# A Mamba-2 mixer that works on two sequences by turns: two transposes and one product change places

## The chip, the cores and the metric

One core of one Trainium2 chip runs the whole kernel. The time is the device time of one execution in microseconds (us), and lower is better. VectorE, ScalarE, GpSimd, TensorE and the DMA queues each run their own list of instructions in order and wait for one another by semaphores.

## The reference

The block has two layers on x of shape (2, 4096, 256). The change lies in the first, a Mamba-2 mixer with a gated linear unit and a layer norm behind it; the second sends each token to 4 of 16 experts.

```
h = layernorm(x) * (1 + ca) + sa
z, xBC, dt = split(h @ W_in)                 # 512, 768, 8 columns
xs, B, C = split(silu(causal_conv4(xBC)))    # 512, 128, 128
state = state * exp(dt*A) + dt * xs (x) B    # 8 heads of 64 x 128, a scan over 4096 tokens
y = state . C + D_skip * xs
y = rmsnorm(y * silu(z)) * rms_w @ W_out + h
a, gate = split(y @ glu_w + glu_b);  y = y + a * sigmoid(gate)
x = x + ga * layernorm(y)
h = layernorm(x) * (1 + cb) + sb             # then the router and the experts
```

The scan is done in chunks of 128 tokens: inside a chunk by a matrix of decays times C.B (tile `dec`), across chunks by the state.

## The kernel before

The kernel has three parts: a first pass over all tokens (layer norm, dt, the sums of the decays), the mixer, and the experts. The mixer takes 256 tokens (two chunks, c = 0 and 1) of one of the two sequences at a time. It is a chain of "halves", written out by hand in `halves`. In a half, up to four groups of tokens are at different stages: `first` (projection and convolution begin), `second` (the scan), `tail` (output projection, gated unit, second norm) and `routed` (third norm, router). From step 4 on every half also has `chosen` or `placed` (the top-4 choice, in the first half of a step, and the assignment of rows, in the second), and `copied` and `sent` (eight indirect stores of 128 rows each on GpSimd's queue, line 1546). Each engine has its own `half` that says in which order it does its share. There are 32 halves with an `add_h`; steps 4 to 15 are twelve of the `chosen` kind and twelve of the `placed` kind, steps 2 and 3 and the half ahead of them have no row stores.

What the steps of this study are, by line:

- VectorE: `add_h` (1308) adds h to the output projection and is the mark from which offsets are counted here. `new_state` (1291) adds a chunk's contribution to the state. `gated` (1313, 1317) makes y of the gated unit, tile `y1`. `norm2` (1323, 1328, 1331) takes mean and variance of the transposed y from PSUM and writes `rs`. `times_decay` (1270) multiplies `dec` by C.B from `bg`. `scale_from_state` (1277), `add_within` (1285), `apply2` (1338, 1345).
- TensorE: `x_by_token` (845) transposes the convolved x of a chunk; `turn_x2` (962) transposes the normalised x of the third norm; `logits` (970) is the router; `b_by_token` (854, 857); `transpose_y2` (951) transposes y of the gated unit; `turn_rows` (982) transposes rows for the stores; `from_state` (905), `state_add` (912), `within` (890, 894).
- ScalarE: `copy_b` (1095) copies C.B and the transposed B to `bg`; `modulate` (1157) follows `turn_x2`.
- GpSimd: `decay_state` (1511) multiplies the state by its decay and stands behind the last six of the eight indirect stores. `shift_x` (1527) stands ahead of them.

The waits that matter:

```
times_decay:       dec_done (chunk c), btok_done          # ScalarE's decays and copy_b
from_state(c=0):   st_done, btok_done
decay_state:       yst_ps                                 # from_state's product
new_state:         add_ps (state_add), sdec_done (decay_state)
transpose_y2:      y2_done (gated), tanh_done
norm2:             y2T_ps (transpose_y2)
turn_x2:           xn_done (normalize), yTl_done, tanh2_done
x_by_token(c):     xs_done, zs_done
```

Of the kernel before, what the change touches and what calls it, by code (L numbers as in the profile page):

```python
# [521 lines left out]
def mixer(nc, sem, prime, clear_semaphores, t, mod, gate_b_row, gate_ln, ident, minus_half, bank, run, h_dram, h2_dram, par_dram,  # L522
          cs_dram, x2_dram, xs_dram):
    with ExitStack() as ctx:
# [184 lines left out]
        def Q(b, n):  # L709
            return bank[4 * b + n]  # L710
# [37 lines left out]
        with nc.Block() as block:  # L748
# [63 lines left out]
            def _(pe):  # L812
# [28 lines left out]
                def x_by_token(b, i, c):  # L841
                    pe.wait_ge(xs_done[b], 3 * i + 2)
                    pe.wait_ge(zs_done[b], CH * i + c + 1)
                    for m in range(KI):
                        last = pe.transpose(Q(b, c)[:, m * P:(m + 1) * P], cv[b][:, m, c * P:(c + 1) * P],
                                            ident[:, :])
                    last.then_inc(xT_ps[b], 1)
# [13 lines left out]
                def exponents(b, i, c):  # L861
                    pe.wait_ge(ends_in[c][b], 32 * (i + 1))
                    if c == 0:
                        pe.wait_ge(xc_done[b], 3 * i + 3)
                        pe.wait_ge(tap0_done[b], 3 * i + 3)
                        pe.wait_ge(st_done[b], CH * i)
                        if above_zero(i - 2):
                            pe.wait_ge(rows_done[b], i - 2)
                        if b == 1 and above_zero(i - 1):
                            pe.wait_ge(pos_read, i - 1)  # L870
                    else:
                        pe.wait_ge(dec_done[b], CH * i + c)

                    for half_heads in range(2):
                        pe.matmul(Q(b, 2 + half_heads)[:, :].rearrange("p (h i) -> p h i", h=4), far[:, :],
                                  after[:, :].unsqueeze(1).to_broadcast([P, 4, P]), start=True, stop=False,
                                  skip_group_check=True)
                    for half_heads in range(2):
                        heads = slice(half_heads * 4, half_heads * 4 + 4)
                        last = pe.matmul(Q(b, 2 + half_heads)[:, :], ends_j[c][:, :],  # L880
                                         ends_i[c][:, heads, :].rearrange("p h i -> p (h i)"),
                                         start=False, stop=True, skip_group_check=True)
                    last.then_inc(dec_ps[b], 1)
# [24 lines left out]
                def state_add(b, i, c):  # L908
                    pe.wait_ge(xend_done[b], CH * i + c + 1)
                    pe.wait_ge(btok_done[b], i + 1)  # L910
                    pe.wait_ge(dec_done[b], CH * i + CH)
                    pe.matmul(Q(b, 3)[:, :], bg[b][:, 0, c, :], xend[b][:, c, :],
                              start=True, stop=True).then_inc(add_ps[b], 1)
# [32 lines left out]
                def transpose_y2(b, i):  # L946
                    pe.wait_ge(y2_done[b], i + 1)
                    pe.wait_ge(tanh_done[b], i + 1)
                    for c in range(CH):
                        for k in range(KD):  # L950
                            last = pe.transpose(Q(b, 1)[:, c * D + k * P:c * D + (k + 1) * P],
                                                y1[b][:, k, c * P:(c + 1) * P], ident[:, :])
                    last.then_inc(y2T_ps[b], 1)
# [48 lines left out]
                def half(first, second, tail, soon=None, routed=None, chosen=None, placed=None, copied=None, sent=None):  # L1002
                    if second:
                        project_z(*second, 1)
                    if tail:
                        project_out(*tail)
                    if second:
                        exponents(*second, 0)
                    if routed:
                        turn_x2(*routed)  # L1010
                    if second:
                        x_by_token(*second, 0)
                        x_by_token(*second, 1)
                    if tail:
                        state_add(*tail, 1)
                    if routed:
                        logits(*routed)
                    if tail:
                        glu(*tail)
                    if second:  # L1020
                        exponents(*second, 1)
                    if first:
                        project_xbc(*first, 0)
                    if second:
                        b_by_token(*second)
                    if tail:
                        transpose_y2(*tail)
                    if copied:
                        turn_rows(*copied)
                    if second:  # L1030
                        from_state(*second, 0)
                        state_add(*second, 0)
                        within(*second, 0)
                        from_state(*second, 1)
                        within(*second, 1)
                    if first:
                        project_xbc(*first, 1)
                        project_xbc(*first, 2)
                    if chosen:
                        positions(*chosen)  # L1040
                    if second:
                        transpose_y(*second, 0)
                    if first:
                        project_z(*first, 0)
                    if second:
                        transpose_y(*second, 1)

                halves(pe, half)


# [180 lines left out]
            def _(dve):  # L1231
# [79 lines left out]
                def gated(b, i):  # L1311
                    dve.wait_ge(tanh_done[b], i + 1)
                    dve.scalar_tensor_tensor(sg[b][:, :, :], sg[b][:, :, :], 1.0, half_a[b][:, :, :],
                                             ALU.add, ALU.mult).then_inc(ag_done[b], 1)
                    dve.wait_ge(ag_done[b], i + 1)
                    dve.wait_ge(y1l_done[b], i + 1)
                    dve.tensor_tensor(y1[b][:, :, :], y1[b][:, :, :], sg[b][:, :, :], ALU.add).then_inc(y2_done[b], 1)
# [117 lines left out]
                def half(first, second, tail, soon=None, routed=None, chosen=None, placed=None, copied=None, sent=None):  # L1435
                    if routed:
                        shift_of_norm3(*routed)
                    if tail:
                        add_h(*tail)
                    if second:  # L1440
                        conv(*second, 2)
                    if tail:
                        new_state(*tail, 1)
                    if second:
                        for c in range(CH):
                            times_dt(*second, c)
                            times_end(*second, c)
                    if chosen:
                        choose(*chosen)
                    if placed:  # L1450
                        assign(*placed)
                    if tail:
                        gated(*tail)
                    if tail:
                        norm2(*tail)
                    if second:
                        times_decay(*second, 0)
                        scale_from_state(*second, 0)
                        new_state(*second, 0)
                        times_decay(*second, 1)  # L1460
                        add_within(*second, 0)
                        scale_from_state(*second, 1)
                    if tail:
                        apply2(*tail)
                    if second:
                        mean_square(*second, 0)
                        add_within(*second, 1)
                    if first:
                        conv(*first, 0)
                    if second:  # L1470
                        mean_square(*second, 1)
                        split_yT(*second, 0)
                    if tail:
                        norm3_stats(*tail)
                    if second:
                        split_yT(*second, 1)
                    if tail:
                        norm3_aggr(*tail)
                    if first:
                        conv(*first, 1)  # L1480
                    if chosen:
                        read_positions(*chosen)

                halves(dve, half)


# [738 lines left out]
```

## Time and profile before

| | us |
|---|---|
| median of 3 runs | 1934.55 (1931.98 to 1934.59) |
| the profiled execution, its own time | 1935.59 |
| its span, first to last instruction | 1933.8 |
| TensorE busy in the span | 1616.6 (84%) |
| VectorE busy | 1336.5 (69%) |
| ScalarE busy | 1114.8 (58%) |
| GpSimd busy | 1000.9 (52%) |

The span is that of one profiled execution; the time of an execution is 1.8 us more than its span. Busy time counts an instruction from its start to its end, and neighbours on one engine overlap by up to some 0.1 us. The mixer's halves begin at about 200 us and the last `add_h` is at 1223.69.

### The profile page before, as it was taken

To read this page: it belongs to the slowest core of one execution; us is meant where nothing else is said; L and a number is where in the kernel's file an instruction comes from. 1 tells how busy PE (TensorE), PEld (TensorE's weight loads), DVE (VectorE), ACT (ScalarE), POOL (GpSimd) and SP (SyncE) were. 2 spreads that over 40 slices of the span, in tenths; PEclk is the share of its full clock that TensorE was granted. 3 is DMA by queue.
4 is the path that set the end of the run, shared out by engine and by line. 5 is a ranking of instruction groups with operands and counts; after the bars stand their busy time and mean duration, and the time that the engine had idled before them with its cause. 6 is when DMAs were issued, how large, how long until landed. Compare 5 with 4: busy or idle time off the path is not lost. (4 is left out here: it accounts for less than half of the span.)

```text
span 1933.8 us, 35775 instructions
## 1 busy us (share of the span) xinstructions
PE 1616.6 (84%) x10868; PEld 1388.4 (72%) x10868; DVE 1336.5 (69%) x3159; ACT 1114.8 (58%) x2270; POOL 1000.9 (52%) x954
## 2 busy tenths in 40 slices
PE   6753999999999999999999999501999999994777
PEld 6743777777777777777777777401999999993554
DVE  6642778888888888888888888414555555552777
ACT  2323575767676767676767676313777776772211
POOL 1201334556566565656565655654566666663432
PEclk8556999999999999999999999655999999997999
DMA  7412011112222121222222211237565665657995
GB/s 250 153 65 63 16 38 36 55 63 74 66 71 69 59 81 59 77 63 70 69 69 69 71 60 66 74 107 225 163 192 182 184 187 180 183 175 261 397 375 211
DMA packets 146311, 238.21 MB, mean 123 GB/s; under 512 B 25644, under 2 KB 92588, under 8 KB 145872
## 3 DMA queue, kind: packets, MB, share of 16 engines
q1 hardware_dynamic: 120016, 164.30, 26.7%
q0 software_dynamic: 26112, 71.62, 10.4%
q8 instruction: 97, 1.59, 0.4%
q14 instruction: 86, 0.70, 0.1%
HBM read 126.36 MB, written 109.48 MB: 122 GB/s over the span
## 5 line engine op out<-in xcount | busy, mean ns | idle before, releaser
L1930 POOL DMA_INDIRECT ys_dram<-byo,bids x272 | 260.8, 959 | 158.2 <-ACT byo L1863 115.3
L1244 DVE SCALAR_TENSOR_TENSOR cv<-xc,convw,cv 128x256 f32<-128x256 f32 x576 | 300.3, 588 | 35.1 <-ACT cv L1071 35.1
L1546 POOL DMA_INDIRECT xs_dram<-rows,dest x256 | 258.0, 1008 | 73.9 <-issue 70.7
L1896 DVE TENSOR_TENSOR bff<-bgs,bank 128x256 f32<-128x256 f32 x136 | 57.2, 421 | 166.4 <-ACT bgs L1847 164.6
L118 PE MATMUL bank<-wh,bhh 128*128 x544 | 157.4, 289 | 1.9 <-issue 1.2
L119 PE MATMUL bank<-wl,bhh 128*128 x544 | 154.8, 284 | 0.0
L120 PE MATMUL bank<-wh,bhl 128*128 x544 | 154.1, 283 | 0.0
L118 PE MATMUL bank<-hTh,win_hi 128*128 128x256 f32 x384 | 116.4, 303 | 36.3 <-POOL hTl L1504 32.9
L1110 ACT ACTIVATE xdt<-yy 128x512 f32<-128x512 f32 x64 | 40.2, 629 | 161.8 <-POOL yy L1517 161.8
L1517 POOL TENSOR_TENSOR yy<-yy,zs 128x512 f32<-128x512 f32 x64 | 87.8, 1371 | 72.4 <-DVE yy L1285 71.9
L1863 ACT ACTIVATE byo<-bank,bx 128x256 f32<-128x256 f32 x272 | 114.1, 471 | 17.1 <-PE bank L120 1.4
L894 PE MATMUL bank<-xdt,dec 128*128 128x64 f32 x1024 | 121.6, 272 | 1.7 <-DVE dec L1270 1.7
L894 PEld LDWEIGHTS bank<-xdt,dec 128*128 128x128 f32 x1024 | 119.5, 192 | 2.1 <-DVE dec L1270 2.1
L1773 PE MATMUL bank<-ident,bx 128*128 128x128 f32 x544 | 83.8, 277 | 36.0 <-DMA bx<-xs_dram 35.9
L1887 DVE TENSOR_TENSOR bhl<-bank,bhh 128x512 fp32r<-128x512 f32 x136 | 94.0, 691 | 26.0 <-ACT bhh L1840 12.1
L118 PEld LDWEIGHTS bank<-hTh,win_hi 128*128 128x128 f32 x384 | 74.1, 193 | 51.4 <-issue 44.7
L120 PE MATMUL bank<-hTh,win_lo 128*128 128x256 f32 x384 | 109.8, 286 | 0.0
L119 PE MATMUL bank<-hTl,win_hi 128*128 128x256 f32 x384 | 109.8, 286 | 0.0
L118 PEld LDWEIGHTS bank<-wh,bhh 128*128 128x128 f32 x544 | 103.3, 190 | 6.5 <-issue 6.1
L1071 ACT ACTIVATE cv<-bank,convb,convw 128x256 f32<-128x256 f32 x192 | 97.6, 562 | 11.4 <-PE bank L120 11.4
L1847 ACT ACTIVATE bgs<-bank 128x256 f32<-128x256 f32 x136 | 52.2, 383 | 89.5 <-PE bank L120 89.5
L119 PEld LDWEIGHTS bank<-wl,bhh 128*128 128x128 f32 x544 | 103.4, 190 | 0.0
(263 smaller groups left out, 5387.3 us busy)
## 6 DMA issues: line engine op xcount, KB each, us to landing
bx<-xs_dram SPq DMA_DIRECT2D x272, 129.0 KB
cy<-ys_dram SPq DMA_DIRECT2D x32, 1024.0 KB, 10.8
px<-in_x SPq DMA_DIRECT2D x16, 512.0 KB, 3.6
h_t<-phT SPq DMA_DIRECT2D x16, 512.0 KB, 4.1
hT<-h_t SPq DMA_DIRECT2D x32, 256.0 KB, 2.7
xr<-in_x SPq DMA_DIRECT2D x32, 256.0 KB, 2.7
x_dram<-xr SPq DMA_DIRECT2D x32, 256.0 KB, 2.0
h_dram<-h SPq DMA_DIRECT2D x32, 256.0 KB, 2.5
```

The source lines that it names most:

```text
L118: pe.matmul(out, a_hi, b_hi, start=start, stop=False, skip_group_check=True)
L119: pe.matmul(out, a_hi, b_lo, start=False, stop=False, skip_group_check=True)
L120: return pe.matmul(out, a_lo, b_hi, start=False, stop=stop, skip_group_check=True)
L894: last = pe.matmul(Q(b, c)[:, h * HD:(h + 1) * HD], dec[b][:, c, h, :], xdt[b][:, c, h * HD:(h + 1) * HD], start=False, stop=True, skip_gr ...
L1071: last = act.activation(cv[b][:, n, :], Q(b, pair)[:, m * GROUP:(m + 1) * GROUP], ACT.Identity, bias=convb[:, n:n + 1], scale=convw[:, n, ...
L1244: dve.scalar_tensor_tensor(cv[b][:, m, :], xc[b][:, m, tap:tap + GROUP], convw[:, m, tap:tap + 1], cv[b][:, m, :], ALU.mult, ALU.add).then ...
L1517: pool.tensor_tensor(y, y, zs[b][:, c, :], ALU.mult).then_inc(y4_done[b], 1)
L1546: pool.indirect_dma_start(out=xs_dram[:, :], out_offset=bass.IndirectOffsetOnAxis(ap=dest[p][:, CH * b + c, k:k + 1], axis=0), in_=rows[b] ...
L1773: last = pe.transpose(XT[u % 2][:, (k * 2 + n) * P:(k * 2 + n + 1) * P], x[u % XBUF][:, n, k * P:(k + 1) * P], ident[:, :])
L1863: last = act.activation(yo[u % YBUF][:, n, :], DN[u % 2][:, n * D:(n + 1) * D], ACT.Copy, scale=x[u % XBUF][:, n, D + 1:D + 2])
L1887: dve.tensor_tensor(hl[u % 2][:, :, :, :].rearrange("p k n t -> p (k n t)"), XT[u % 2][:, :], hh[u % 2][:, :, :, :].rearrange("p k n t -> ...
L1930: pool.indirect_dma_start(out=ys_dram[:, :], out_offset=bass.IndirectOffsetOnAxis(ap=ids[u % XBUF][:, n:n + 1], axis=0), in_=yo[u % YBUF][ ...
```

## The change

Three steps change places, in TensorE's and VectorE's order of work. No instruction, tile or wait is added or taken away.

- TensorE turns the normalised x (`turn_x2`) between the two `x_by_token` and no longer ahead of both.
- TensorE turns y (`transpose_y2`) behind `turn_rows`, the first `from_state` and the first `state_add`, and no longer ahead of the three.
- VectorE does the first `times_decay` ahead of `norm2` and no longer behind it.

```diff
--- before.py
+++ after.py
@@ -1006,10 +1006,11 @@
                         project_out(*tail)
                     if second:
                         exponents(*second, 0)
+                    if second:
+                        x_by_token(*second, 0)
                     if routed:
                         turn_x2(*routed)
                     if second:
-                        x_by_token(*second, 0)
                         x_by_token(*second, 1)
                     if tail:
                         state_add(*tail, 1)
@@ -1023,13 +1024,14 @@
                         project_xbc(*first, 0)
                     if second:
                         b_by_token(*second)
+                    if copied:
+                        turn_rows(*copied)
+                    if second:
+                        from_state(*second, 0)
+                        state_add(*second, 0)
                     if tail:
                         transpose_y2(*tail)
-                    if copied:
-                        turn_rows(*copied)
-                    if second:
-                        from_state(*second, 0)
-                        state_add(*second, 0)
+                    if second:
                         within(*second, 0)
                         from_state(*second, 1)
                         within(*second, 1)
@@ -1451,10 +1453,11 @@
                         assign(*placed)
                     if tail:
                         gated(*tail)
+                    if second:
+                        times_decay(*second, 0)
                     if tail:
                         norm2(*tail)
                     if second:
-                        times_decay(*second, 0)
                         scale_from_state(*second, 0)
                         new_state(*second, 0)
                         times_decay(*second, 1)
```

## Rows read from the trace of the kernel before

**Rows 1.** Busy time by stage, mixer: us, each engine's busy us (count), PEclk, DMA.
```profile
200.00:1224.00 1024.00, 952.69 (x6435) 790.31 (x6435) 866.32 (x2083) 708.74 (x1405) 581.23 (x554) 0.99 0.19 62
```

**Rows 2.** Timeline, VectorE, a chosen half: start, us, line, tiles, [idle before].
```profile
700.00 0.69 DVE L1308 TENSOR_TENSOR y<-bank,hT 128x512 f32<-128x512 f32 x1 [0.41 <-PE bank L120]
...
711.80 0.69 DVE L1317 TENSOR_TENSOR y<-y,sg 128x512 f32<-128x512 f32 x1
...
713.24 0.76 DVE L1323 BATCH_NORM_STATS2 st<-bank 128x6 f32<-128x256 f32 x2 [0.75 <-PE bank L951]
...
714.43 0.17 DVE L1331 TENSOR_SCALAR rs<-mv 128x2 f32<-128x2 f32 x1
...
714.51 1.22 DVE L1270 TENSOR_TENSOR dec<-dec,bg 128x1024 f32<-128x1024 f32 x1
...
715.65 0.68 DVE L1277 TENSOR_TENSOR yy<-bank,par 128x512 f32<-128x512 f32 x1
...
716.74 0.69 DVE L1291 TENSOR_TENSOR state<-state,bank 128x512 f32<-128x512 f32 x1 [0.41 <-POOL state L1511]
...
733.14 0.69 DVE L1308 TENSOR_TENSOR y<-bank,hT 128x512 f32<-128x512 f32 x1 [0.27 <-PE bank L120]
```

**Rows 3.** Timeline, GpSimd, the same half.
```profile
712.91 0.96 POOL L1546 DMA_INDIRECT xs_dram<-rows,dest  x1 [0.30 <-issue]
...
714.17 0.96 POOL L1546 DMA_INDIRECT xs_dram<-rows,dest  x1 [0.30 <-issue]
...
715.15 1.48 POOL L1511 TENSOR_TENSOR state<-state,par 128x512 f32<-128x512 f32 x1
```

**Rows 4.** Timeline, ScalarE and TensorE, the same half.
```profile
711.17 0.60 ACT L1095 ACTIVATE bg<-bank 128x512 f32<-128x512 f32 x1 [1.04 <-PE bank L857]
...
712.55 0.66 PE L951 MATMUL bank<-ident,y 128*128 128x128 f32 x4 [1.42 <-DVE y L1317]
```

**Rows 5.** Timeline, VectorE, the half behind it.
```profile
746.45 1.23 DVE L1270 TENSOR_TENSOR dec<-dec,bg 128x1024 f32<-128x1024 f32 x1
...
749.69 0.69 DVE L1291 TENSOR_TENSOR state<-state,bank 128x512 f32<-128x512 f32 x1 [1.42 <-POOL state L1511]
...
765.25 0.69 DVE L1308 TENSOR_TENSOR y<-bank,hT 128x512 f32<-128x512 f32 x1 [0.41 <-PE bank L120]
```

**Rows 6.** Timeline, GpSimd, the same half.
```profile
744.84 0.96 POOL L1546 DMA_INDIRECT xs_dram<-rows,dest  x1 [0.30 <-issue]
...
747.37 1.14 POOL L1546 DMA_INDIRECT xs_dram<-rows,dest  x1 [0.30 <-issue]
...
748.53 1.05 POOL L1511 TENSOR_TENSOR state<-state,par 128x512 f32<-128x512 f32 x1
```

**Rows 7.** Timeline, VectorE and TensorE, an early half without row stores.
```profile
277.31 0.69 DVE L1308 TENSOR_TENSOR y<-bank,hT 128x512 f32<-128x512 f32 x1 [0.41 <-PE bank L120]
...
289.23 1.10 PE L905 MATMUL bank<-state,cv 128*128 128x512 f32 x2 [0.34 <-ACT bg L1095]
...
291.02 1.05 PE L890 MATMUL bank<-skip_w,cv 128*128 128x128 f32 x8
...
292.42 0.69 DVE L1291 TENSOR_TENSOR state<-state,bank 128x512 f32<-128x512 f32 x1 [0.40 <-POOL state L1511]
...
308.28 0.69 DVE L1308 TENSOR_TENSOR y<-bank,hT 128x512 f32<-128x512 f32 x1 [0.41 <-PE bank L120]
```

**Rows 8.** Timeline, VectorE and GpSimd, four instructions where the two meet.
```profile
322.16 1.04 POOL L1511 TENSOR_TENSOR state<-state,par 128x512 f32<-128x512 f32 x1 [6.41 <-PE bank L905]
...
322.44 0.79 DVE L1331 TENSOR_SCALAR rs<-mv 128x2 f32<-128x2 f32 x1
...
648.23 2.63 DVE L1270 TENSOR_TENSOR dec<-dec,bg 128x1024 f32<-128x1024 f32 x1
...
709.49 0.41 DVE L1391 TENSOR_SCALAR mask<-mask 128x64 f32<-128x64 f32 x1
```

**Rows 9.** Timeline, TensorE's weight loads, the router's first.
```profile
703.38 0.19 PEld L970 LDWEIGHTS bank<-gatew,h 128*128 128x128 f32 x1 [0.39 <-ACT h L1157]
```

More of the change, by code:

```diff
@@ L1025, in half @@
                         b_by_token(*second)
-                    if tail:
-                        transpose_y2(*tail)
                     if copied:
@@ L1032, in half @@
                         state_add(*second, 0)
+                    if tail:
+                        transpose_y2(*tail)
+                    if second:
                         within(*second, 0)
```

## The prediction

> **What bounds the kernel now.** I read the busy time by stage first. The mixer takes 1024 of the 1934 us, at full granted clock, with TensorE busy 93% and VectorE 85% [rows 1]. Neither is idle for long, so shares decide nothing here; what decides is which wait ends last inside a half. So I laid the timelines of the engines side by side. The reader is to look at the idle time in brackets. In the half from 700.00 to 733.14 VectorE waits 0.41 us ahead of `new_state`, until GpSimd has decayed the state [rows 2]; in the next half it waits 1.42 us at the same place [rows 5]. GpSimd itself is not waiting there: `decay_state` starts 0.02 us after the end of the last indirect store, 715.15 after 714.17 + 0.96 [rows 3], and 748.53 after 747.37 + 1.14 [rows 6]. So from `add_h` to the first `new_state` the half is set by GpSimd's queue of stores, and VectorE and TensorE have some slack on the way. Behind `new_state` everything hangs on VectorE's order: from it to the next `add_h` it is 733.14 - 716.74 = 16.40 us in a `chosen` half and 765.25 - 749.69 = 15.56 us in a `placed` half [rows 2, 5]. I keep these two as they are and ask only where the first `new_state` goes. Offsets below count from `add_h` of the half. Before, `new_state` is at 16.74 (chosen) and 16.55 (placed).
>
> **First swap, turns of x.** `turn_x2` waits for ScalarE, and one `x_by_token` could fill that gap. But the router comes two steps later, and its first weight load waits 0.39 us for `modulate` [rows 9], which stands in ScalarE's own order. What TensorE gains ahead of it, it waits there. I cost the swap at 0; its cover is that wait. Were turn_x2 late by a transposition or two, the bound is some 0.1 us a half on a path that has the slack above. I take nothing for either sign.
>
> **TensorE turns y later.** `from_state` needs `bg`, whose copy ends at 11.17 + 0.60 = 11.77 [rows 4]. In the early half `from_state` starts 11.92 after `add_h` on that same copy, and two steps later the next product starts at 291.02 - 277.31 = 13.71 [rows 7]. Now `transpose_y2` takes that slot, in every half, for y is ready before (12.49 in a chosen half [rows 2]; in a placed one 746.45 less norm2's 1.27 and the 0.75 of turning, offset 11.29 [rows 2, 5]). Statistics start 713.24 - 712.55 = 0.69 after the turning starts [rows 2, 4], so at 14.40, where they were at 13.24. `rs` is written at +1.19, at 15.59, and the next product starts at +1.27, at 15.67 (714.43, 714.51 against 713.24 [rows 2]). That next product is now `scale_from_state`, 0.68 us, so VectorE alone could start `new_state` at 16.35. Before in the chosen half it could at 15.65 + 0.68 = 16.33. So the later turning costs no VectorE time where stores set the pace: -0.39 in a chosen half and -0.20 in a placed one would be possible if GpSimd came earlier.
>
> **Where there are no stores the turning costs.** In the three plain halves of this kind `new_state` was at 292.42 - 277.31 = 15.11 and now comes at 16.35. The rest of the half was 15.86 [rows 7] and can shrink to the placed half's 15.56, for TensorE is no longer late. Each is between 0.94 and 1.24 longer, I take 1.0: +3.0. The four mixed halves at the two ends (two chosen, two placed, with none or few stores) gain on the one kind and lose on the other; I take +0.2 each, +0.8, with bounds of -0.4 and +1.0 each.
>
> **The product moved ahead meets the stores.** This is the term that decides. The rows read as if VectorE's product of two SBUF tiles and GpSimd's work shared one thing that only one can hold; I call it the port. The `dec` product 714.51 to 715.73 stretches `decay_state` from 715.15 to 1.48 us against 1.05 in the placed half, where VectorE waits [rows 2, 3, 6]: it ends 0.90 after the product. The product 746.45 to 747.68 stretches the store at 747.37 to 1.14 against 0.96: it ends 0.83 after the product [rows 5, 6]. But a `dec` product that begins 0.34 into a store (714.51 against 714.17) stretches nothing. A store then needs the port at some moment between 0.13 (0.96 - 0.83) and 0.34 after its start.
>
> *Chosen half.* The product now runs from 12.49 to 13.71 and frees `decay_state` of its 0.43. But the store at 12.91 stands in it: it ends at 13.71 + 0.83 = 14.54 and not at 13.87, so the last store and `decay_state` shift by some 0.65, to 14.8 and 15.80 [rows 3]. An undisturbed `decay_state` is followed by `new_state` 1.16 after its start (749.69 - 748.53 [rows 5, 6]): 16.96, or +0.2.
>
> *Placed half.* y is ready, so the product waits for `bg` and starts some 0.03 behind its end, at 11.80. The store before it starts at 744.84 - 733.14 = 11.70 [rows 5, 6]. It has started, and needs the port not before +0.13, at 11.83. I take it that the product, 0.03 ahead, wins: it holds the port till 13.02, the store ends at 13.85 and not at 12.66, +1.19. The last store loses its 0.18, for no product stands there any more. `decay_state` goes from 15.39 to 16.40 and `new_state` to 17.56, +1.0. The bounds of this term are 0 (no meeting) and 1.2 (a whole product).
>
> The Trainium skill has a rule on this ("SBUF — State Buffer", section "SBUF: two separate sides"): VectorE and GpSimd share one pair of ports as an exclusive lock, and whichever instruction starts first has it to its end. The two stretched rows agree; the `dec` product inside a store does not, for it neither waited nor stretched anything. By the rule as written the store at 11.70 would win, which is rival C below.
>
> **Sum.** 12 x 0.2 + 12 x 1.0 + 3.0 + 0.8 = 18.2. One chosen half has a `dec` product of 2.63 us against 1.22 [rows 8], a meeting with `decay_state` that the new place makes impossible: -1.2. Total +17. The profiled execution took 1935.6, which is 1.0 above the median of the runs; I predict 1951 for the median.
>
> **Rivals.**
>
> *A', the statistics lose the port too.* A small `tensor_scalar` is held by GpSimd: `rs` took 0.79 us, until `decay_state` was over (322.44 + 0.79 = 323.23, 322.16 + 1.04 = 323.20), and another took 0.41 inside a store, until its end [rows 8]. In a chosen half `rs` at 15.59 now stands inside the last store (14.8 to 15.8) with `decay_state` 0.02 behind it. If it misses the gap it ends at 16.85, `scale_from_state` with it, and `new_state` is at about 17.4, 0.45 more than in the sum: +5.4, 1956. For it: the 2.63 us product is one that missed such a gap. Against it: that is one case in twelve.
>
> *B, the store reads first in the placed half.* Then the product is late by 0.2 at most, the next store at 12.96 is stretched by 0.0 to 0.16, and `decay_state` starts at 15.2 to 15.4, ahead of `rs` at 15.59, which it holds to its end. `scale_from_state` ends some 0.6 behind that and `new_state` is at 16.85 to 17.0: +0.4 in place of +1.0, and the total is +10: 1944. The two moments lie 0.03 apart, so this is nearly as likely.
>
> *C, the store holds the port to its end.* The product of the placed half starts at 12.66 and ends at 13.88, the store at 12.96 ends at 14.71 and not at 13.92, `decay_state` starts at 16.0: +0.6, and the total is +12: 1947.
>
> *D, the other side: no price at the ports.* If the stores find their moment between products, `new_state` comes at 16.35 in both kinds: -0.39 and -0.20, together -7.1, with +3.8 at the ends and -1.2: -4.5, which is 1930. It decides as soon as the product moved ahead stretches the stores by less than the 0.43 by which it frees `decay_state`. Against it: four stretched rows and a store that lies squarely inside the product's new place.
>
> *E, nothing.* Slack swallows all of it: within 4 us of 1934.
>
> **Chances.** The sum's case 0.33, A' 0.12, B 0.22, C 0.10, D 0.09, E and the unforeseen 0.14. A measurement of this kernel can't tell less than 0.2% (3.9 us) from no change. Faster comes from D, less a part of it that is inside 3.9 us, and some of the unforeseen: 0.09. Same: E and the rest of D: 0.12. Slower 0.79. For the range I leave out D and E and keep A' and B with the unknown of the placed term: 1937 to 1958. The likeliest case's own range is 1947 to 1954.
>
> **What would show it.** The first `times_decay` of a chosen half starts right behind y, at 12.5, and the store at 12.9 takes some 1.6 us in place of 0.96. In a placed half `times_decay` starts at 11.80 and the store at 11.70 takes 2.1 us (B: 0.96; C: 0.96 with the product late). `decay_state` takes 1.05 in both kinds. `norm2` starts at 14.40 in every half. VectorE's wait for `decay_state` stays in both kinds, and the periods are 33.4 (chosen) and 33.1 (placed). Router and gated unit stand where they stood. The prediction is wrong if the stores are not stretched, or if the rest of a half behind `new_state` is not the 16.40 and 15.56 of before.

## The result and the profile after

The changed kernel takes 1953.95 us in the median of 4 runs (1951.43 to 1959.53), the kernel before 1934.57 beside it (4 runs, 1931.98 to 1938.84). The ratio is 1.010, with an interval of 1.0072 to 1.0128: slower by 14 to 25 us. The forecast was 1951. The profiled execution of after took 1951.43, with a span of 1949.5, which is 15.7 us above the span of before.

The views of after, in the order in which the prediction went through before. First the busy time by stage (us, busy us and count of TensorE, its weight loads, VectorE, ScalarE and GpSimd, then granted clock, DMA share, GB/s), and the first and the last `add_h`:

```profile
200.00:1240.00 1040.00, 968.36 (x6420) 794.32 (x6418) 886.29 (x2083) 709.59 (x1408) 577.91 (x555) 0.99 0.19 61
...
212.99 0.69 DVE L1310 TENSOR_TENSOR y<-bank,hT 128x512 f32<-128x512 f32 x1 [0.84 <-PE bank L120]
...
1237.61 0.69 DVE L1310 TENSOR_TENSOR y<-bank,hT 128x512 f32<-128x512 f32 x1 [4.27 <-PE bank L120]
```

From the first `add_h` to the last it is 1024.62 us, and it was 1008.13 in the trace of before (215.56 to 1223.69): +16.5. The stretch ahead of it is 2.6 shorter and the one behind it 1.8 longer. The traces of the first group below, with the same code in these two stretches, differ by as much (212.5 to 216.1 and 702 to 713). So what this trace shows of the change lies in the mixer's halves. Its 16.5 us are some 3 less than the 19.4 between the two medians.

One `chosen` half, from 704.41 to 738.14 (33.73 us; [rows 2] had 33.14). VectorE's timeline:

```profile
704.41 0.69 DVE L1310 TENSOR_TENSOR y<-bank,hT 128x512 f32<-128x512 f32 x1 [0.41 <-PE bank L120]
...
716.83 1.22 DVE L1272 TENSOR_TENSOR dec<-dec,bg 128x1024 f32<-128x1024 f32 x1
...
718.59 0.76 DVE L1325 BATCH_NORM_STATS2 st<-bank 128x6 f32<-128x256 f32 x2 [0.55 <-PE bank L951]
...
719.78 1.48 DVE L1333 TENSOR_SCALAR rs<-mv 128x2 f32<-128x2 f32 x1
...
721.77 0.67 DVE L1293 TENSOR_TENSOR state<-state,bank 128x512 f32<-128x512 f32 x1
...
738.14 0.69 DVE L1310 TENSOR_TENSOR y<-bank,hT 128x512 f32<-128x512 f32 x1 [0.27 <-PE bank L120]
```

GpSimd's timeline of the same half, where [rows 3] showed before:

```profile
717.32 1.56 POOL L1549 DMA_INDIRECT xs_dram<-rows,dest  x1 [0.30 <-issue]
...
719.18 0.96 POOL L1549 DMA_INDIRECT xs_dram<-rows,dest  x1 [0.30 <-issue]
...
720.17 1.05 POOL L1514 TENSOR_TENSOR state<-state,par 128x512 f32<-128x512 f32 x1
```

The product at offset 12.42 stretches the store at 12.91 to 1.56, and `decay_state` comes at 15.76 for 1.05, as forecast (15.80). But VectorE has no wait ahead of `new_state` any more. It is busy with `rs`, two columns wide, which took 0.17 before [rows 2] and takes 1.48 now: it begins inside the last store and ends at 721.26, with `decay_state` (721.22). `new_state` is at 17.36, and not at 16.96.

The `placed` half behind it, 738.14 to 770.46 (32.32 us), VectorE and GpSimd:

```profile
749.85 1.23 DVE L1272 TENSOR_TENSOR dec<-dec,bg 128x1024 f32<-128x1024 f32 x1 [0.44 <-ACT bg L1097]
...
753.51 0.91 DVE L1333 TENSOR_SCALAR rs<-mv 128x2 f32<-128x2 f32 x1
...
754.93 0.67 DVE L1293 TENSOR_TENSOR state<-state,bank 128x512 f32<-128x512 f32 x1
...
770.46 0.69 DVE L1310 TENSOR_TENSOR y<-bank,hT 128x512 f32<-128x512 f32 x1 [0.41 <-PE bank L120]
```
```profile
749.83 0.96 POOL L1549 DMA_INDIRECT xs_dram<-rows,dest  x1 [0.30 <-issue]
...
752.35 0.96 POOL L1549 DMA_INDIRECT xs_dram<-rows,dest  x1 [0.30 <-issue]
...
753.32 1.06 POOL L1514 TENSOR_TENSOR state<-state,par 128x512 f32<-128x512 f32 x1
```

Store and product begin 0.02 apart, and neither is longer than when alone: 0.96 and 1.23. The stores run off undisturbed, `decay_state` comes at 15.18 (before 15.39 [rows 5, 6]), and here too it holds `rs`, to 754.42. `new_state` is at 16.79; before it was at 16.55.

Where the 16.5 us come from, by kind of half (sums of the periods from `add_h` to `add_h`):

| halves | before | after | | forecast |
|---|---|---|---|---|
| 12 `chosen` | 399.40 | 411.10 | +11.7 | +1.2 (12 x 0.2 - 1.2) |
| 12 `placed` | 385.16 | 388.05 | +2.9 | +12.0 |
| 3 plain | 92.72 | 94.68 | +2.0 | +3.0 |
| 4 mixed | 130.85 | 130.79 | -0.1 | +0.8 |

Of the twelve `chosen` halves seven take 33.7 us, and five take 34.9 to 35.1. The windows of one of the five (it begins at 437.77) show what is different:

```profile
452.00:454.00 2.00, 2.00 (x21) 2.00 (x20) 1.82 (x5) 1.08 (x4) 1.67 (x3) 1.00 0.18 66
454.00:456.00 2.00, 0.68 (x6) 0.54 (x6) 2.00 (x4) 0.00 (x0) 1.31 (x2) 1.00 0.18 66
456.00:458.00 2.00, 2.00 (x5) 0.97 (x5) 1.72 (x3) 0.00 (x0) 0.38 (x1) 0.52 0.00 0
458.00:460.00 2.00, 2.00 (x14) 2.00 (x13) 1.97 (x5) 0.72 (x2) 0.90 (x1) 0.63 0.00 0
460.00:462.00 2.00, 2.00 (x20) 2.00 (x20) 0.89 (x4) 0.72 (x1) 0.55 (x1) 1.00 0.38 139
```

The granted clock falls to about half (1.2 of 2.4 GHz) for some 3 us, and five instructions fill 2 us of TensorE where twenty did. It falls behind an idle stretch: the second `from_state` waits for the late `new_state`.

```profile
455.86 1.92 PE L905 MATMUL bank<-state,cv 128*128 128x512 f32 x2 [1.32 <-DVE state L1293]
```

All twelve `chosen` halves have an idle stretch of about this length (1.30 to 1.35, and once 1.51), and seven keep the clock. The five that lose it begin at 437.77, 571.10, 836.53, 970.08 and 1103.40, which is every other one from the second on, with one left out (704.41). In the halves of after the second `from_state` takes over 1.3 us in these five alone (1.54 to 2.07), in before in none. The clock also falls in the last mixed half, but it does so in both kernels, with the first `from_state` at 2.05 and 1.92. Between 500 and 1200 us VectorE's `new_state` keeps TensorE waiting 24.0 us in sum, at most 1.6 at once; before it was 6.6 and 0.8 (table of waits: engine, line, what it waited for; sum, times, longest; before has line 1291, after 1293):

```profile
PEld bank L905 <- DVE state L1291: 6.6, 10, 0.8
```
```profile
PEld bank L905 <- DVE state L1293: 24.0, 21, 1.6
```

### The profile page after: what moved, and what is told of

It reads as the page before. It is cut to its first block and busy times, and to the rows that moved or that the text cites. A ratio compares the mean times of both kernels' runs of the same rounds, so it can differ in the third digit from the quotient of the medians.

```text
span 1949.5 us, 35775 instructions
## 1 busy us (share of the span) xinstructions
PE 1631.7 (84%) x10868; PEld 1391.5 (71%) x10868; DVE 1356.3 (70%) x3159; ACT 1114.2 (57%) x2270; POOL 998.0 (51%) x954
## 5 line engine op out<-in xcount | busy, mean ns | idle before, releaser
L1549 POOL DMA_INDIRECT xs_dram<-rows,dest x256 | 263.9, 1031 | 73.6 <-issue 69.1
L118 PE MATMUL bank<-hTh,win_hi 128*128 128x256 f32 x384 | 115.9, 302 | 40.2 <-POOL hTl L1507 33.1
L905 PE MATMUL bank<-state,cv 128*128 128x512 f32 x128 | 75.7, 675 | 38.2 <-DVE state L1293 25.3
## 6 DMA issues: line engine op xcount, KB each, us to landing
cy<-ys_dram SPq DMA_DIRECT2D x32, 1024.0 KB, 10.8
```

Of the source, the lines that this page charges most:

```text
L118: pe.matmul(out, a_hi, b_hi, start=start, stop=False, skip_group_check=True)
L1549: pool.indirect_dma_start(out=xs_dram[:, :], out_offset=bass.IndirectOffsetOnAxis(ap=dest[p][:, CH * b + c, k:k + 1], axis=0), in_=rows[b] ...
```

## The experiments

Twelve runs were made in three groups, each group on a chip of its own together with the kernel before. On the first chip that kernel takes 1936.5 us, on the second 2109.4, on the third 2061.4. So a ratio holds only inside its group, and behind the first group the experiments are read half by half. The changed kernel itself was not in the first group: its 1953.95 us and the ratio of 1.010 come from the run of the result, where before took 1934.57. On the other two chips the kernel before has times but no trace.

### First group: which part does what

**One swap alone, the turns of x.**

```diff
+                    if second: x_by_token(*second, 0)
                     if routed: turn_x2(*routed)
-                    if second: x_by_token(*second, 0)
```

> Only the first swap, of the two turns of x; y is turned and the product made where the kernel before does. In the changed kernel `bg` is copied 0.16 us earlier (offset 11.01 against 11.17), which only this swap can have brought. Theory Q (GpSimd's queue of stores sets the first `new_state`): halves with stores keep their periods of 33.14 and 32.09, the three plain halves give 0.2 each, total within 1 us of the kernel before. Rival T (TensorE's order sets the half): 31 x 0.16 = 5 us faster, 1929.5.

1936.35 us (10 runs), ratio 1.0008, 0.9984 to 1.0033: no change. `copy_b` now comes at offset 10.99 and not at 11.17 [rows 4]:

```profile
701.78 0.69 DVE L1309 TENSOR_TENSOR y<-bank,hT 128x512 f32<-128x512 f32 x1 [0.41 <-PE bank L120]
...
712.77 0.60 ACT L1096 ACTIVATE bg<-bank 128x512 f32<-128x512 f32 x1 [1.04 <-PE bank L857]
```

The plain halves take 30.80 in place of 30.98; the halves with stores stay at 33.15 and 32.08, for there GpSimd sets `new_state`. One half takes 35.95: its `dec` product takes 2.63, like that of [rows 8], and then the second `from_state` 1.92, so the clock can fall with y still turned early. The swap isn't quite the 0 that it was costed at: it is worth 0.18 us of `bg`, and only where no stores are.

**The later turn of y alone.**

```diff
-                    if tail: transpose_y2(*tail)
                     turn_rows, from_state(0), state_add(0)
+                    if tail: transpose_y2(*tail)
```

> Only the later turning of y on TensorE; VectorE still does `norm2` ahead of the first product. Theory Q: the product can't start before norm2 is over at 15.7, or 16.2 where `rs` is held by `decay_state`, so `new_state` comes at 18.1 in both kinds (+1.3 and +1.5) and TensorE idles for some 2 us ahead of `within`, so that the granted clock falls in most halves (about 1.2 each): 1975 to 2010. Rival P (the loss of the change comes from where the product stands): no slower than the changed kernel, 1951.

2060.26 us (4 runs), ratio 1.0658, 1.0612 to 1.0703. It is by far the costliest single step, and dearer than either theory had it. With the product still behind `norm2`, the product comes at 16.2 and `new_state` at 17.9 in both kinds. What TensorE waits for is the product, ahead of the first `within`, and not `new_state`; the clock falls in 20 of the 24 halves with stores. TensorE's longest wait and windows of 4 us from one of them:

```profile
1070.92 2.83 PE L894 MATMUL bank<-xdt,dec 128*128 128x64 f32 x16 [2.26 <-DVE dec L1271]
```
```profile
1066.00:1070.00 4.00, 2.66 (x16) 1.70 (x14) 2.01 (x6) 2.94 (x7) 3.25 (x5) 1.00 0.28 101
1070.00:1074.00 4.00, 3.08 (x17) 3.07 (x18) 3.33 (x5) 0.00 (x0) 1.45 (x1) 0.74 0.00 0
1074.00:1078.00 4.00, 4.00 (x15) 2.98 (x14) 2.91 (x7) 0.72 (x2) 1.26 (x1) 0.50 0.00 0
1078.00:1082.00 4.00, 4.00 (x33) 4.00 (x33) 2.21 (x4) 1.46 (x3) 1.93 (x2) 0.91 0.40 135
```

The rest of a half behind `new_state` grows from 16.4 and 15.6 to 19.7 and 19.3 us in most halves; in the four where the clock stays up it is 16.5 and 16.0. So the expectation had the delay (18.1) and the fall of the clock, but priced a fall at 1.2 us where it costs some 3.2.

**The product ahead of the statistics, alone.**

```diff
+                    if second: times_decay(*second, 0)
                     if tail: norm2(*tail)
-                    if second: times_decay(*second, 0)
```

> Only the first decay product ahead of `norm2`; TensorE's order is the one before. Theory Q: in a chosen half the store at 12.9 is stretched to 1.56 and `decay_state` starts at 15.77, but `rs` is written at about 14.8, ahead of it, so `new_state` is at 16.93 (+0.2); in a placed half nothing is stretched and it is at 16.36 (-0.2). With no 2.63 us product: 1931 to 1935, the same as before. Rival P (the moved product is what costs): chosen halves 0.6 longer, 1942 or more.

1934.12 us (10 runs), ratio 0.9993, 0.9973 to 1.0013: no change, as expected. The trace shows both meetings with the stores without the later turn. Chosen half (`add_h` at 695.53), GpSimd, then VectorE:

```profile
708.45 1.56 POOL L1547 DMA_INDIRECT xs_dram<-rows,dest  x1 [0.31 <-issue]
...
711.29 1.05 POOL L1512 TENSOR_TENSOR state<-state,par 128x512 f32<-128x512 f32 x1
```
```profile
707.95 1.22 DVE L1270 TENSOR_TENSOR dec<-dec,bg 128x1024 f32<-128x1024 f32 x1
...
710.27 0.24 DVE L1331 TENSOR_SCALAR rs<-mv 128x2 f32<-128x2 f32 x1
...
712.45 0.69 DVE L1291 TENSOR_TENSOR state<-state,bank 128x512 f32<-128x512 f32 x1 [1.35 <-POOL state L1512]
```

Placed half (`add_h` at 728.85), GpSimd, then VectorE:

```profile
740.53 0.96 POOL L1547 DMA_INDIRECT xs_dram<-rows,dest  x1 [0.30 <-issue]
741.80 0.99 POOL L1547 DMA_INDIRECT xs_dram<-rows,dest  x1 [0.31 <-issue]
```
```profile
740.73 1.23 DVE L1270 TENSOR_TENSOR dec<-dec,bg 128x1024 f32<-128x1024 f32 x1 [0.61 <-ACT bg L1095]
```

In the chosen half `new_state` comes at 16.92, what the sum had for the whole change (16.96), with 1.35 us of VectorE idle: the stretched store sets it. `rs` ends before `decay_state` begins and pays nothing. So the sum's +0.2 was right for the stores, and what after has on top (17.36) is `rs` in its later place. That holds for eleven of the twelve: in the half from 629.85 `rs` begins 0.36 late, at 15.10, is held for 1.76 by the last store and `decay_state`, and `new_state` comes at 17.38. In the placed half the product starts 0.20 into a store and stretches nothing, and `new_state` comes at 16.39, 0.16 earlier than before. The two kinds cancel: by their periods +1.2 and -2.1 us.

**The changed kernel with spare work ahead of the second `from_state`**, in the `chosen` halves. `fill` turns eight tiles of `cv` into a bank that is free; nothing reads them.

```diff
                         within(*second, 0)
+                        if chosen: fill(*second)   # 8 transposes, 1.05 us
                         from_state(*second, 1)
```

> The changed kernel with eight spare transposes (0.9 us, into a bank that is overwritten next) on TensorE ahead of the second `from_state`, in chosen halves only, where TensorE waits 1.3 us. Theory C (the idle TensorE loses its clock in some of the twelve chosen halves, 1.16 us each): the granted clock stays 1.00 in all of them, their periods are all 33.74, the time is 5 x 1.16 = 5.8 us below the profiled execution of the changed kernel, 1946, and the spread of its executions (1951.4 to 1959.5) is gone. Rival N: the low clock has another cause; 5 of 12 stay at 34.9 and the time is 1951 to 1959.

1938.45 us (10 runs), ratio 1.0015, 0.9998 to 1.0032. The changed kernel had 1.010, beside other runs of before and in 4 runs of its own; the intervals lie apart. The expected 1946 is missed by 7.5 us, and the spread has not gone (1934.5 to 1945.9). TensorE's timeline and the windows around the same place:

```profile
454.41 1.05 PE L904 MATMUL bank<-ident,cv 128*128 128x128 f32 x8
...
455.88 1.13 PE L912 MATMUL bank<-state,cv 128*128 128x512 f32 x2 [0.43 <-DVE state L1302]
```
```profile
455.00:457.00 2.00, 1.57 (x9) 0.86 (x7) 2.00 (x4) 0.00 (x0) 0.44 (x1) 1.00 0.00 0
457.00:459.00 2.00, 2.00 (x21) 2.00 (x20) 1.97 (x5) 0.06 (x1) 1.27 (x1) 1.00 0.00 0
```

The idle stretch is 0.43 and no longer 1.32, the clock stays up in all twelve, and all take 33.74 to 33.98. The mixer takes 1018.1, 6.5 less than in the trace of after; five falls of 1.16 were 5.8. That is what the trace shows of the clock's price. The rest of the drop in the median is not explained: 1.0100 less 1.0015 of 1936 us is 16.4, 10 more than the profiled mixers differ. In this trace the part behind the mixer took 701.8 us, where the other traces of this chip show 708 to 713. Each execution's mean granted clock is on record too. It is 0.913 to 0.918 in the four of after, 0.918 to 0.923 in 25 of before and 0.919 to 0.922 in the ten with spare work, and the slowest execution of after (1959.53) has the lowest. So after has less clock throughout, and in some executions less than in the profiled one (0.917). How much of the 10 us that is was not worked out.

### Second and third group: the stores and `rs`

The changed kernel was repeated in both.

> The changed kernel unaltered, on the same chip as the next three and in more executions. Its first 4 executions were spread over 1951.4 to 1959.5 us, and in the profiled one the granted clock fell in 5 of the 12 chosen halves, at 1.16 us each. Theory C (the number of such halves differs from one execution to the next): the number in this profile need not be 5, and the mixer's length is 1018.8 + 1.16 x that number. Rival: it is fixed by the program, 5 again in the same halves.

> The changed kernel unaltered once more, beside the next three. On the chip of the group before, where the kernel before took 2109 us, both kernels stood for some 3 us a half in TensorE waiting for nothing but its own instructions, ahead of the first `from_state`, and the two took the same time. Theory C: on a chip where the kernel before takes some 1935 us the changed one takes 14 to 22 us more, by the number of chosen halves in which the clock falls (0 to 12, 1.16 us each).

Second chip: 2105.21 (10 runs), ratio 0.9974, 0.9948 to 1.0001. Third: 2072.42 (10 runs), ratio 1.0053, 1.0025 to 1.0081. So the cost is not the same on every chip; the 14 to 22 us that were expected where before takes 1935 were not tested, for neither chip is of that kind. The count of falls could not be tested either: the mixers take 1072.4 and 1056.2 us, far from 1018.8 and 1.16 for each fall, and the clock falls at other places too. The plain halves are as on the first chip (31.52 to 31.62). But in many of the halves with stores ScalarE's `copy_b`, on which `from_state` and the product wait, comes up to 5.1 us late, and TensorE stands ahead of the first `from_state` for up to 4.6 us. The trace names no engine of this core as the releaser (table of waits, second chip, 500 to 1200 us):

```profile
PEld bank L905 <- issue: 50.7, 20, 4.6
...
ACT bg L1097 <- remote: 36.1, 9, 5.1
```

I call it the unnamed wait. A half that waits there anyway should pay less for a late product or `rs`; that this is why the ratio is smaller is argued and not shown, without a trace of before there. The part behind the mixer takes 799 to 808 us on these chips and some 710 on the first. Neither is explained.

**`rs` behind `new_state`, in the changed kernel.**

```diff
                     if tail: norm2(*tail)              # without rs
                     if second:
                         scale_from_state(*second, 0)
                         new_state(*second, 0)
+                    if tail: add_eps2(*tail)           # rs
```

> The changed kernel with one instruction moved: the small `tensor_scalar` that writes `rs` in `norm2` (a third part of it) comes behind the first `new_state`, where GpSimd has no longer anything to hold it with. Theory R (in every half with stores `rs` waits for `decay_state`, and all behind it on VectorE too): `new_state` goes to `decay_state` + 1.16, 16.93 in a chosen half and 16.36 in a placed one, each 0.44 earlier; TensorE then waits less and its clock stays at 1.00, which is 5.8 us more. About 16 us below the changed kernel less some 0.1 us a half for the instruction's new place: 1938 to 1943. Rival S (the stretched store is what costs): 1951 or more.

> The changed kernel with the small `tensor_scalar` that writes `rs` behind the first `new_state`, again. As before: `new_state` at 16.93 (chosen) and 16.36 (placed) in place of 17.36 and 16.80, clock at 1.00 all through, 10 to 16 us below the changed kernel. Rival S (only the stretched store costs): the same as the changed kernel.

Second chip: 2096.1 (5 runs), ratio 0.994, 0.9919 to 0.9962, beside 0.9974 for the changed kernel. Third: 2071.06 (10 runs), ratio 1.004, 1.0008 to 1.0073, beside 1.0053. In the whole time it can't be told from the changed kernel there, so the 10 to 16 us of the expectation did not show. In halves with little of the unnamed wait it can be told, where `copy_b` comes equally late in both (at 11.9 in a chosen half, 11.1 to 11.2 in a placed one): on the third chip `new_state` is at 17.05 to 17.11 (chosen) and 16.36 to 16.47 (placed), where the changed kernel has 17.51 to 17.61 and 16.82 to 16.89. A placed half, VectorE:

```profile
611.39 0.69 DVE L1310 TENSOR_TENSOR y<-bank,hT 128x512 f32<-128x512 f32 x1 [0.28 <-PE bank L120]
...
627.77 0.69 DVE L1293 TENSOR_TENSOR state<-state,bank 128x512 f32<-128x512 f32 x1 [0.30 <-POOL state L1519]
628.38 0.16 DVE L1335 TENSOR_SCALAR rs<-mv 128x2 f32<-128x2 f32 x1
```

`rs` takes 0.16 again and `new_state` waits for GpSimd again: 0.4 to 0.5 us of delay of `new_state` are shown to be its hold. The halves are 0.3 to 0.4 us shorter, for `rs` takes some 0.1 in its new place.

**Six of the eight stores ahead of `decay_state`, two behind GpSimd's half**, so that `decay_state` comes earlier: on the changed kernel, on the kernel before, and on before with the x swap and the product ahead of the statistics but y turned where it was.

```diff
-                        scatter(*sent, slice(2, 8))
+                        scatter(*sent, slice(2, 6))
 ...                     # the rest of GpSimd's half
+                    if sent: scatter(*sent, slice(6, 8))
```

> The changed kernel with the last two of the six indirect stores moved from ahead of `decay_state` to the end of GpSimd's half, where it waits. Theory Q (the stores set the first `new_state`): `decay_state` starts at 12.9, `rs` at 15.37 is free, `new_state` comes at 16.05 in both kinds, the halves take 32.4 and 31.6 as in the early ones without stores, the clock stays up: mixer about 1001, 1927. Rival: the later turning of y alone costs, the stores are no matter: 1951.

> The kernel before with two of the six stores moved to the end of GpSimd's half and nothing else. Theory Q: in a placed half `decay_state` follows `from_state` at 13.38, is held by the product to 15.4, and the half takes 31.3 as the one early placed half did (-0.8); in a chosen half `decay_state` could start at 14.58 but the product from 14.51 holds it to 16.6, so 33.1 stays: 10 us less, 1925. Rival: the stores are not what sets `new_state`: 1935.

> The version that the runs so far point to: the first product ahead of `norm2` and the swap of the turns of x as in the change, but y is turned where it was before, and two of the six stores come at the end of GpSimd's half. Theory Q: as in the early halves of the run with the product alone, 32.3 (chosen) and 31.3 (placed) with `new_state` at about 15.5 and 15.0, where TensorE's own work is the next limit: 12 x 0.8 + 12 x 0.8 + 1.2 + some 1 = 21 us below the kernel before, 1914. Rival: the two stores at the end delay the second `decay_state` or the third norm's root by what they gain: 1930 or more.

> Product ahead of `norm2`, swap of the turns of x, y turned where it was before, two stores at the end of GpSimd's half, again. Theory Q: with `decay_state` free of both stores and product, 32.3 (chosen) and 31.0 to 31.3 (placed): 20 us below the kernel before, 1914, and about 10 below the kernel before with the stores split alone, since only here is the product out of `decay_state`'s way. Rival: no faster than with the stores split alone.

| kernel | chip | us (runs) | ratio to before | interval |
|---|---|---|---|---|
| changed, split | second | 2068.73 (4) | 0.979 | 0.9753 to 0.9826 |
| before + x swap + product, split | second | 2038.57 (4) | 0.9673 | 0.9645 to 0.97 |
| before, split | third | 2021.23 (4) | 0.9809 | 0.9757 to 0.986 |
| before + x swap + product, split | third | 2016.19 (4) | 0.978 | 0.9726 to 0.9833 |

All three are faster than both kernels of this study, by 40 to 71 us where 10 to 21 were expected. The halves gain what was expected and no more: with the split alone the placed ones take 31.3 in nine of twelve (31.3 expected, 32.09 in before on the first chip) and most chosen ones 33.25 (33.1 expected). That is some 10 us. The other 30 can't be placed, for the kernel before has no trace on these chips. The unnamed wait may be in them: between 500 and 1200 us `copy_b` waits 3.5 us in it in the trace of before with the split, and 22.4 in that of the changed kernel on the same chip. The mixer of the last row takes 1001.3 us in its trace, that of the third 1006.0, while the changed kernel's takes 1056.2 on that chip.

The first two rows differ in one thing, the place where y is turned. The later place costs 30 us there, and the intervals lie apart. So y turned late costs also where the stores no longer set `decay_state`. In a placed half of before with the split the product still meets `decay_state` (GpSimd, then VectorE):

```profile
612.58 1.83 POOL L1511 TENSOR_TENSOR state<-state,par 128x512 f32<-128x512 f32 x1 [1.02 <-PE bank L905]
```
```profile
598.88 0.69 DVE L1308 TENSOR_TENSOR y<-bank,hT 128x512 f32<-128x512 f32 x1 [0.27 <-PE bank L120]
...
612.28 1.23 DVE L1270 TENSOR_TENSOR dec<-dec,bg 128x1024 f32<-128x1024 f32 x1
...
614.51 0.69 DVE L1291 TENSOR_TENSOR state<-state,bank 128x512 f32<-128x512 f32 x1 [0.41 <-POOL state L1511]
```

and with the product ahead of the statistics it no longer does:

```profile
612.97 1.04 POOL L1513 TENSOR_TENSOR state<-state,par 128x512 f32<-128x512 f32 x1 [0.76 <-PE bank L905]
```
```profile
599.57 0.69 DVE L1309 TENSOR_TENSOR y<-bank,hT 128x512 f32<-128x512 f32 x1 [0.27 <-PE bank L120]
...
611.36 1.23 DVE L1271 TENSOR_TENSOR dec<-dec,bg 128x1024 f32<-128x1024 f32 x1 [0.52 <-issue]
...
614.55 0.67 DVE L1292 TENSOR_TENSOR state<-state,bank 128x512 f32<-128x512 f32 x1
```

`new_state` goes from 15.63 to 14.98, but both halves take 31.3: TensorE's order now sets them. The chosen halves missed their expectation of 32.3 (33.0 to 33.1 in six, the others longer). There the first `from_state` is at 13.5, directly behind the turning of y, which is ready at 12.5; the second follows at 17.84 without a gap. In the kernel before it is at 13.48 as well, and the early half on which the 32.3 rested has it at 12.77. In the whole time the two can't be told apart on the third chip (2016 and 2021, intervals overlap). None of the split kernels ran on a chip where before takes 1935.

## Why the prediction was right, and where its working was not

The direction and the size were right: +17 forecast, +16.5 in the mixer's halves and +19.4 by the medians. Where in the mixer it would fall was wrong: +12.0 was put on the placed halves and +1.2 on the chosen ones, and they took +2.9 and +11.7. Errors of both signs made up the sum.

- **The x swap, costed at 0**: nearly. It brings `bg` 0.18 earlier, which in e1 no half with stores could use.
- **Statistics at 14.40, VectorE's own `new_state` at 16.35**: 14.18 in the chosen half, and 16.05 in a plain one; of the 0.22 and 0.30 some 0.18 is the swap's. The plain halves cost 2.0 and not 3.0, as their `new_state` is 0.3 earlier than forecast.
- **Chosen half, the store stretched by 0.65 and `decay_state` at 15.80 for 1.05**: right (stretch 0.60, 15.76, 1.05). The step that failed is the one behind it, that `new_state` follows 1.16 later: `rs` missed the gap of 0.03 between the last store and `decay_state`, in all twelve chosen halves (1.13 to 1.68 us), not in one of them. This is rival A', at its own price (17.36, forecast 17.4). The late `rs` comes from the later turn: with the product moved and y turned early, it costs nothing in eleven halves of twelve. Price: 12 x 0.6 = 7.2, where the sum had 2.4.
- **Placed half, the product wins over the store**: wrong, and the largest error. The forecast had the product 0.10 behind the store (11.80 and 11.70) and read from the stretched rows that the store needs the port not before 0.13. The traces show that a product must begin 0.044 or more ahead of a store to hold it. In after it begins 0.00 to 0.03 behind it, so the price of a whole product was missed by 0.04 to 0.07 us. It is rival B, with `new_state` at 16.8 as B had it (16.85 to 17.0), and `rs` held by `decay_state`: +0.24 each, +2.9 against +12.
- **The 2.63 us product is gone**: right. No half of after has one.
- **A term that was missing**: the granted clock. I kept the rest of a half at 16.40 and 15.56. It is so in the placed halves (15.5) and in seven chosen ones (16.4). In five it is 17.5, for the idle stretch ahead of the second `from_state` has grown to 1.3 us: 5.8 us in this execution. With the spare work in that stretch they go. [Rows 1] with a clock of 0.99 over the stage gave no warning, but the prediction moved `new_state` later and never asked who waits for it on TensorE.
- **Both errors together**: 7.2 - 1.2 + 5.8 (11.8 in the chosen halves), 2.9, 2.0 and -0.1 are +16.6, with +16.5 measured. Without the clock, A' and B at their measured prices make +10.8. The +12 of the placed halves that didn't come was replaced by terms that the sum didn't have, so that +17 was hit is largely luck.

The rule of the Trainium skill ("SBUF — State Buffer", section "SBUF: two separate sides") that whichever instruction starts first has the shared ports to its end would have put C in the placed half. The trace disagrees: a product beginning 0.02 behind a store took 1.23. For `rs` of the placed half, which begins 0.19 behind `decay_state`, it agrees, with ends 0.04 apart. In the chosen half `rs` begins ahead of `decay_state` and still ends with it, 0.04 behind.

What stays open: why equal idle stretches take the clock in five halves and leave it in seven, how often in other executions, and so how much of the 19 us of the medians is the clock's; the unnamed wait on the two slower chips, and what the split gains there beyond 10 us; the changed kernel in one group with the spare work, and with `rs` moved, on a chip where before takes 1935; and the split kernels there.

## What to carry to other kernels

When a reordering makes an instruction later, ask not only whether it still beats the wait that ends last, but what it will then overlap: a two-column instruction of 0.17 us cost a half 0.4 to 0.5, only by starting while GpSimd was busy. Follow the delay to TensorE as well, for an idle stretch there can cost more than its own length. And where a queue sets the pace, try to move work out of the queue: taking two stores from ahead of `decay_state` gained 1.9 to 3.3% on two chips, though only some 10 us of it are seen in the halves and none of it was measured on the first. A sum that comes out right is no proof of its terms: compare each kind of half.

## What the runs showed of the hardware

- An indirect store and VectorE's product of two SBUF tiles: a store that begins inside the product ends 0.83 or 0.84 after it, at most 0.89 (1.56 us in place of 0.96 in after and e3). A product that begins 0.03 to 0.4 into a store is not held and holds nothing. The border is sharp over the fourteen traces: a product that begins 0.044 us or more ahead of a store holds it; one that begins 0.043 ahead or less leaves it at 0.96 and is itself held a little, 1.30 us in place of 1.23 at 0.043 ahead and 1.25 when both begin together. So the store has what it needs within some 0.03 us of its start.
- The small `tensor_scalar` is different: it is held by the store's later part and through the operation behind it, for 1.48 us. On the third chip it took 0.16 behind `new_state`.
- Behind idle stretches of TensorE of 1.3 to 1.5 us the granted clock fell to about 0.5 for some 3 us in five of twelve alike halves. With 0.43 to 0.63 us it did in none of twelve (e5), and with 0.8 us in none of the twelve placed halves of after. One fall cost 1.16 us. Behind waits of 2.26 us (the later turn alone) it cost some 3.2 us in most halves.
- The same kernel before takes 1936, 2061 and 2109 us on three chips, each with one group of runs.
